# Last self-attention: V held still in the weighing, one group later, with one exponential per head

## The chip, the core and the metric

The kernel runs on one core of a Trainium2 chip. The metric is the device time of one execution in microseconds (us), the smaller the better. TensorE multiplies (PE in the rows, PEld its weight loads), VectorE is DVE, ScalarE is ACT, GpSimd is POOL and SyncE issues DMAs (SP).

## What is computed

A Perceiver block of two layers on x (128 batches of 32 tokens of 256 numbers): in each layer a cross-attention to a context of 257 tokens, a self-attention and a feed-forward part. The change touches only the second layer's self-attention (16 heads of 64, causal, rotary embedding), which the kernel runs in one stage with the quantised linear layer that ends the program:

```python
def _L1_attn_ref(x, W_qkv, W_out):          # x: (128, 32, 256), after a layer norm
    q, k, v = split(x @ W_qkv)              # 16 heads of 64
    q, k = rotary(q), rotary(k)
    scores = einsum('bqhd,bkhd->bhqk', q, k) / 8
    scores = where(tril, scores, -1e9)
    weights = softmax(scores)
    out = einsum('bhqk,bkhd->bqhd', weights, v)
    return out.reshape(b, s, 1024) @ W_out
x = x + _L1_attn_ref(_layernorm(x), ...)
x = x + _L1_ffn_ref(_layernorm(x), L1_ffn_weight)   # BitLinear: rounded rows times a ternary matrix
```

## The kernel before

The program is five stages, one after the other: cross-attention, self-attention with the router, experts, cross-attention, and the last stage (class `SelfAttention1`, from 1971 us of the profile to its end). Tokens lie on the 128 partitions, four batches of 32 in one group; there are G = 32 groups. The last stage walks over them in steps. Each engine has its own list of instructions, written out by hand in the methods `tensor`, `scalar`, `vector` and `gpsimd`, and meets the others only in semaphores, so an instruction that waits holds back all that stands behind it on its engine.

In the kernel before, step g holds: for group g, six projections to 512 columns (q in two halves, k in two, v in two; `project(g, i, c)`, each 6 products of 128 rows to 512 columns by way of `split_product`, L230), the rotary product (`rotate` on VectorE, three instructions at L2333 and L2336; the sum on GpSimd, L2407), the turning of the rotated q and k (`turn`, four transposes each, L2198) and copies of them by ScalarE (L2284); for group g-1 the scores (`scores`, L1131, 64 products in tiles of 64 rows by 32 columns of the array), the softmax and the weighing (`weigh`, L1180, in tiles of 32 by 32, the turned probabilities standing still and V streaming past in 64 columns); for group g-2 the turning of the result (`turn_out`, L2211), its split into a high and a low part (`attn_hi` on ScalarE, L2291, `attn_lo` on VectorE, L2345), and the output projection (`project_out`, 24 products of 256 columns, L230); and for older groups the BitLinear part: row statistics, rounding, two transposes (L2090) and two products (L2107), with `add` on VectorE (L2114). An f32 product appears in the trace as two matmuls, so 64 products are 128 records.

The softmax is all VectorE but for the exponential: two masked reads of the scores (L1151), the maximum (L1156), the subtraction (L1158), one exponential of 512 columns on ScalarE (L1137), the block transpose (L1164), the sums (L1165) and their reciprocal (L1171). After the weighing VectorE multiplies the 1024 columns of the result by the reciprocals (L2392, 1024 columns), and this is what `turn_out` waits for.

PSUM: two banks for the scores, two for the weighed result, and a ring of four banks for everything else. Whoever takes a bank of the ring waits until its last user but four takes ago has been read: `Ring.take` keeps that order, which is the order of the takes in `tensor`. Order of TensorE in a middle step before: q0, q1, turn_out 0, k0, k1, turn_out 1, turn q0, turn q1, scores(g-1), v0, turn k0, project_out(g-2), turn k1, v1, bit transposes, weigh(g-1), bit product. Layer norm of four groups is made ready in every fourth step (8 more transposes there).

## Time and profile before

| | us |
|---|---|
| median of three runs | 2590.14 |
| lowest, highest | 2585.91, 2591.77 |
| the profiled execution | 2589.96 |
| its span, first to last instruction | 2587.8 |
| mean granted TensorE clock of the span | 0.965 of full speed |
| scores of group 0 and of group 31 begin | 1996.7, 2549.3 |

The rows further down come from the profiled execution. A window row gives for a stretch its length, then the busy time and number of instructions of PE, PEld, DVE, ACT and POOL, the granted clock, the share of the DMA engines and GB/s. A group row gives the line, the engine, what is written from what, the shape, the count, the busy time and the mean length in ns, and behind the second bar the idle time of the engine before these instructions and what ended it. A timeline row gives start and length in us, and in brackets an idle time before it.

### The profile page before, as it was taken

The page shows a single profiled execution, that of the slowest core. Times are in us where ns is not written, and L with a number is a line of the kernel's source. Part 1 is how long each engine was busy: PE and PEld are TensorE (multiplying, and loading weights), DVE is VectorE, ACT ScalarE, POOL GpSimd, SP SyncE. Part 2 cuts the span into 40 slices and gives each one's busy share as a digit, 9 for nine tenths or more (in the row PEclk, how much of TensorE's full clock was granted, in tenths as well). Part 3 has the DMA queues.
Part 4 walks back from the last instruction along what each step waited for, and adds up shares of the span by engine and source line. Part 5 has one row for each costly group of instructions (what it writes and reads, how often), then busy time and mean ns, then how long its engine had stood idle before and what let it go on. Part 6 is the DMA issues. An engine that isn't in the chain of part 4 may idle for free. (4 is left out here: it accounts for less than half of the span.)

```text
span 2587.8 us, 103372 instructions
## 1 busy us (share of the span) xinstructions
PE 2402.1 (93%) x44640; PEld 1977.3 (76%) x44640; DVE 1813.0 (70%) x3820; ACT 1252.9 (48%) x2824; POOL 840.0 (32%) x740
## 2 busy tenths in 40 slices
PE   7999999999988857999995999999997999999997
PEld 6888888888855546888884777777776888888885
DVE  6778777777767663222225888888886788888886
ACT  5666666666544433333334777777763223232332
POOL 3333333332222112343435444444221323233231
PEclk9999999999998867999998999999998999999998
DMA  6545555554323253111115788888772000000000
GB/s 203 145 147 158 156 157 152 159 153 127 98 57 103 75 198 144 49 50 47 50 39 168 221 233 232 237 227 234 218 208 91 3 3 3 11 11 11 11 11 26
DMA packets 199554, 298.98 MB, mean 116 GB/s; under 512 B 29368, under 2 KB 107324, under 8 KB 197824
## 3 DMA queue, kind: packets, MB, share of 16 engines
q1 hardware_dynamic: 192288, 275.58, 36.0%
q0 software_dynamic: 6816, 16.79, 2.0%
q8 instruction: 356, 5.83, 1.0%
q14 instruction: 94, 0.77, 0.1%
HBM read 170.75 MB, written 78.77 MB: 96 GB/s over the span
## 5 line engine op out<-in xcount | busy, mean ns | idle before, releaser
L813 ACT ACTIVATE prob_x<-ps_score_x,neg_max_x 128x257 f32<-128x257 f32 x1024 | 402.6, 480 | 202.1 <-DVE neg_max_x L880 202.0
L880 DVE TENSOR_REDUCE neg_max_x<-ps_score_x 128x2 f32<-128x514 f32 x512 | 328.7, 683 | 109.8 <-PE ps_score_x L697 108.9
L708 PEld LDWEIGHTS ps_v_x<-v_wide_x,probT_x 128*32 128x32 f32 x18432 | 287.5, 108 | 129.3 <-issue 125.4
L708 PE MATMUL ps_v_x<-v_wide_x,probT_x 128*32 128x68 f32 x18432 | 335.0, 223 | 27.3 <-issue 23.1
L904 DVE STREAM_TRANSPOSE probT_x<-prob_x 128x1152 f32<-128x1152 f32 x256 | 343.8, 1343 | 0.0
L1049 POOL TENSOR_TENSOR ctxT_x_lo<-ready,ctxT_x_hi 128x514 fp32r<-128x514 f32 x128 | 152.9, 1195 | 387.0 <-ACT ctxT_x_hi L792 345.6
L2407 POOL TENSOR_TENSOR rot_s<-turned_s,swapped_s 128x512 f32<-128x512 f32 x128 | 164.5, 1297 | 328.0 <-DVE swapped_s L2336 288.2
L1049 POOL TENSOR_TENSOR split<-loaded,split 128x514 fp32r<-128x514 f32 x128 | 153.4, 1199 | 334.3 <-ACT split L792 319.9
L230 PE MATMUL ps_x<-split,w_q_x_hi 128*128 128x258 f32 x1024 | 208.5, 300 | 21.3 <-DVE w_q_x_lo L274 18.7
L230 PEld LDWEIGHTS ps_x<-split,w_q_x_hi 128*128 128x128 f32 x1024 | 160.0, 192 | 42.0 <-issue 25.9
L1947 DVE TENSOR_TENSOR hid_moe<-ps_up_moe,silu_moe 128x512 f32<-128x512 f32 x71 | 49.1, 691 | 203.5 <-PE ps_up_moe L230 203.5
L697 PE MATMUL ps_score_x<-kT_x,q_x 32*64 32x257 f32 x4096 | 178.2, 401 | 13.2 <-ACT prob_x L813 9.6
L804 ACT ACTIVATE kT_x<-ps_x,bias_k 128x257 f32<-128x257 f32 x256 | 122.1, 478 | 127.0 <-PE ps_x L230 126.5
L896 DVE STREAM_TRANSPOSE v_x<-ps_x 128x288 f32<-128x288 f32 x256 | 121.3, 479 | 74.6 <-PE ps_x L230 74.0
L230 PE MATMUL ps_x<-ctxT_x_hi,w_v_x_hi 128*128 128x258 f32 x512 | 159.0, 311 | 10.5 <-POOL ctxT_x_lo L1049 10.5
L230 PE MATMUL ps_x<-ctxT_x_hi,w_k_x_hi 128*128 128x258 f32 x512 | 146.4, 286 | 7.7 <-DVE v_x L896 7.7
L2291 ACT ACTIVATE attnT_s_hi<-ps_s 128x512 fp32r<-128x512 f32 x64 | 38.1, 599 | 231.4 <-PE ps_s L2211 231.4
L230 PE MATMUL ps_x<-split,w_q_x_lo 128*128 128x258 f32 x512 | 146.5, 286 | 0.0
L230 PE MATMUL ps_x<-ctxT_x_hi,w_v_x_lo 128*128 128x258 f32 x512 | 145.0, 283 | 0.0
L230 PE MATMUL ps_x<-ctxT_x_lo,w_v_x_hi 128*128 128x258 f32 x512 | 145.0, 283 | 0.0
L230 PE MATMUL ps_x<-ctxT_x_lo,w_k_x_hi 128*128 128x258 f32 x512 | 145.0, 283 | 0.0
L230 PE MATMUL ps_x<-ctxT_x_hi,w_k_x_lo 128*128 128x258 f32 x512 | 144.5, 282 | 0.0
(293 smaller groups left out, 6000.5 us busy)
## 6 DMA issues: line engine op xcount, KB each, us to landing
v_wide_x<-v_x SPq DMA_DIRECT2D x512, 76.5 KB, 2.1
v_out_x<-v_x SPq DMA_DIRECT2D x128, 306.0 KB, 4.2
v_wide_x<-v_out_x SPq DMA_DIRECT2D x512, 76.5 KB, 3.1
ready<-ctx SPq DMA_DIRECT2D x128, 257.0 KB, 3.6
loaded<-ctx SPq DMA_DIRECT2D x128, 257.0 KB, 4.2
gate_whole<-moe_experts SPq DMA_DIRECT2D x32, 256.0 KB, 3.8
lo_out<-gate_whole SPq DMA_DIRECT2D x32, 256.0 KB
w_moe<-lo_out SPq DMA_DIRECT2D x8, 1024.0 KB, 8.5
```

Source lines behind the costliest of these rows:

```text
L230: last = pe.do.matmul(out, a, b, start=n == 0, stop=n == len(steps) - 1)
L697: ins = pe.do.matmul(self.ps[m * 2 * T:(m + 1) * 2 * T, r, 0:S], q, self.kT[b % 3][rows, m, 0:S], start=True, stop=True)
L708: ins = pe.do.matmul(self.ps_v[r * T:(r + 1) * T, b % 2, :, :], self.probT[b % 3][:, r, n * T:(n + 1) * T], self.v_wide[b % 4][:, :, r, n, ...
L804: act.do.activation(out, src, ACT.Identity, bias=self.biases["k"][:, m:m + 1]).then_inc(*s.k.at(tag, b, m))
L813: act.do.activation(self.prob[b % 3][:, r, 0:S], self.ps[:, r, 0:S], ACT.Exp, bias=self.neg_max[b % 2][:, r:r + 1]).then_inc(*s.exp.at(tag ...
L880: dve.do.tensor_reduce(self.neg_max[b % 2][:, r], self.ps[:, r, 0:S], AX_X, ALU.max, negate=True).then_inc(*s.neg_max.at(tag, b, half))
L896: dve.do.transpose(out.rearrange("p x n d -> p n x d"), src.rearrange("p (n x d) -> p n x d", x=2, d=XD)).then_inc(*s.v.at(tag, b, m))
L904: dve.do.transpose(flat(self.probT[b % 3]), flat(self.prob[b % 3])).then_inc(*s.prob_T.at(tag, b))
L1049: pool.do.tensor_tensor(self.ctxT[b % 3].lo[:, :, 0:S], self.ctx_in[g % 2][:, j, :, :], self.ctxT[b % 3].hi[:, :, 0:S].bitcast(F32), ALU.s ...
L1947: dve.do.tensor_tensor(self.hid[t % 2][:, :], self.up_ps[t % 2][:, :], self.silu[t % 2][:, :], ALU.mult).then_inc(*s.hid.at(t))
L2291: act.do.activation(self.attnT.hi[:, c * 512:(c + 1) * 512], banks["attn", g, c][:, :], ACT.Copy).then_inc(*s.a_hi.at(g, c))
L2407: pool.do.tensor_tensor(self.rot[e][:, :, :], self.turned[e][:, :, :], self.swapped[e][:, :, :], ALU.add).then_inc(*s.r_rot.at(g, i, c))
```

## The change

- The softmax is cut in three. `mask` (VectorE) does the masked reads and the maximum. `exponent` (ScalarE) does one exponential per head, 16 of 32 columns, with the negative maximum as bias and with the sum of the head written out by the same call. `divide` (VectorE) takes the reciprocal of the sums, multiplies the 512 probabilities and does the block transpose. The subtraction (L1158), the sums (L1165) and the product over 1024 columns (L2392) are gone.
- `weigh` lets V stand still (32 rows by 64 columns) and streams the turned probabilities (32 columns): tiles of 32 by 64. Its result is already turned, so `turn_out` (eight transposes a step) is gone, and `attn_hi` and `attn_lo` read the weighed result itself.
- The weighed result of a group takes half of each of four banks; the other halves of two of these are the scores. So `mask` waits for the end of the weighing, and scores and reads of the result are kept apart by waits.
- Order: a step opens on TensorE with scores(g-1), then weigh(g-2), which was weigh(g-1) near the end of the step; then q0, q1, k0, k1, v0, turn q0, turn q1, project_out(g-2), turn k0, turn k1, bit transposes, v1, bit product. ScalarE and VectorE follow with their new lists. The ring of four banks is taken in the new order.
- The DMAs, the products of the projections and GpSimd's list are as before.

The diff, cut to its core:

```diff
@@ -1119,66 +1118,65 @@
         return a.rearrange("p (r n) -> p r n", r=self.order.R)
 
     def scores(self, pe, g, q_k):
-        s, tag, R = self.s, self.tag, self.order.R
+        s, R = self.s, self.order.R
         if g:
-            if self.bound is None:
-                pe.wait_ge(s.s_shift, tag, g - 1)
-            else:
-                pe.wait_ge(s.s_masked, g - 1)
+            pe.wait_ge(s.s_masked, g - 1)
         for heads, q, k in q_k(g):
             for b in range(BPG):
                 for r in range(R):
                     ins = pe.do.matmul(self.score[b * T:(b + 1) * T, r, heads, :], q(b, r), k(b, r), start=True, stop=True)
-        ins.then_inc(*s.s_score.at(tag, g))
+        ins.then_inc(*s.s_score.at("s1", g))
+
+    def mask(self, dve, g):
+        s, t, e = self.s, self.t, g % 2
+        dve.wait_ge(s.s_score, "s1", g)
+        if g >= 2:
+            dve.wait_ge(s.s_exp, "s1", g - 2)
+        for r in range(self.order.R):
+            ins = dve.do.scalar_tensor_tensor(out=self.cell(t["shifted"][e][:, :])[:, r], in0=self.score[:, r], scalar=self.scale,
+                                              in1=self.bound.unsqueeze(1).to_broadcast([P, self.order.NH, T]), op0=ALU.mult, op1=ALU.min)
+        ins.then_inc(*s.s_masked.at(g))
+        dve.wait_ge(s.s_masked, g)
+        dve.do.tensor_reduce(self.stat(t["neg_max"][e][:, :]), self.cell(t["shifted"][e][:, :]), AX_X, ALU.max, negate=True).then_inc(
+            *s.s_max.at("s1", g))
 
     def exponent(self, act, g):
-        s, tag, e = self.s, self.tag, g % 2
-        act.wait_ge(s.s_shift, tag, g)
-        act.do.activation(self.t["prob"][e][:, :], self.t["shifted"][e][:, :], ACT.Exp,
-                          scale=self.scale if self.bound is None else 1.0).then_inc(*s.s_exp.at(tag, g))
+        s, t, e = self.s, self.t, g % 2
+        act.wait_ge(s.s_max, "s1", g)
         if g >= 2:
+            act.wait_ge(s.s_probT, "s1", g - 2)
+            act.wait_ge(s.s_inv, "s1", g - 2)
+        for n in range(H):
+            own = slice(n * T, (n + 1) * T)
+            ins = act.do.activation(t["prob"][e][:, own], t["shifted"][e][:, own], ACT.Exp, bias=t["neg_max"][e][:, n:n + 1],
+                                    accum_out=t["sums"][e][:, n:n + 1])
+        ins.then_inc(*s.s_exp.at("s1", g))
+
+    def divide(self, dve, g):
+        s, t, e = self.s, self.t, g % 2
+        by_head = lambda a: a.rearrange("p (h q) -> p h q", q=T)
+        dve.wait_ge(s.s_exp, "s1", g)
+        dve.do.reciprocal(t["inv"][e][:, :], t["sums"][e][:, :]).then_inc(*s.s_inv.at("s1", g))
+        dve.wait_ge(s.s_inv, "s1", g)
+        dve.do.tensor_tensor(by_head(t["prob"][e][:, :]), by_head(t["prob"][e][:, :]),
+                             t["inv"][e][:, :].unsqueeze(2).to_broadcast([P, H, T]), ALU.mult).then_inc(*s.s_even.at(g))
+        dve.wait_ge(s.s_even, g)
         if g >= 2:
+            dve.wait_ge(s.s_pv, "s1", g - 2)
+        dve.do.transpose(t["probT"][e][:, :], t["prob"][e][:, :]).then_inc(*s.s_probT.at("s1", g))
 
     def weigh(self, pe, g, out, v, dv):
+        s, probT = self.s, self.t["probT"][g % 2]
+        pe.wait_ge(s.s_probT, "s1", g)
+        for n in range(H // 2):
+            for x in range(2):
+                h = 2 * n + x
+                c0 = self.order.column[h]
+                for b in range(BPG):
+                    rows = slice(b * T, (b + 1) * T)
+                    ins = pe.do.matmul(out[x * dv:(x + 1) * dv, b, n, :], v[rows, h * dv:(h + 1) * dv], probT[rows, c0:c0 + T],
+                                       start=True, stop=True)
+        ins.then_inc(*s.s_pv.at("s1", g))
 
...
         self.R = R = P // D1
-        order = HeadOrder(R, lambda r, n: n * R + r, lambda a: a.rearrange("p (n r) -> p r n", r=R))
-        ps_score = stack.enter_context(nc.psum_tensor(f"ps_score_{tag}", [P, R, 512], F32))
-        ps_out = stack.enter_context(nc.psum_tensor(f"ps_out_{tag}", [P, F1], F32))
+        order = HeadOrder(R, lambda r, n: n * R + r)
+        halves = stack.enter_context(nc.psum_tensor(f"ps_halves_{tag}", [P, BPG, 512], F32))
         self.banks = Ring([stack.enter_context(nc.psum_tensor(f"ps_{i}_{tag}", [P, 512], F32)) for i in range(4)])
-        self.out = ps_out[:, :].rearrange("p (h d) -> p h d", d=D1)
-        self.soft = SelfSoftmax(s, tag, order, self.t, ps_score[:, :, 0:order.NH * T].rearrange("p r (n q) -> p r n q", q=T),
+        self.out = halves[:, :, 256:512].rearrange("p b (n q) -> p b n q", q=T)
+        self.soft = SelfSoftmax(s, order, self.t, halves[:, 0:R, 0:order.NH * T].rearrange("p r (n q) -> p r n q", q=T),
...
+    def out_part(self, c):
+
+        return self.out[:, 2 * c:2 * c + 2, :, :]
+
+    def attn_part(self, t, c):
+
+        return t[:, :].rearrange("p (n b q) -> p b n q", n=H // 2, q=T)[:, 2 * c:2 * c + 2, :, :]
 
...
         def project_out(g):
             bank, emptied = banks.take(("o", g), s.s_x1, g)
-            pe.wait_ge(s.a_hi, g, self.NB - 1)
-            pe.wait_ge(s.a_lo, g, self.NB - 1)
+            pe.wait_ge(s.a_hi, g, 0)
+            pe.wait_ge(s.a_lo, g, 0)
             if emptied:
                 pe.wait_ge(*emptied)
             self.wout.await_split(pe)
...
             if g == 2:
                 self.bit.sum_weight(pe)
+            if before:
+                pe.wait_ge(s.r_qkT, g - 1, 1, self.NB - 1)
+                if g >= 3:
+                    pe.wait_ge(s.a_lo, g - 3, 0)
+                self.soft.scores(pe, g - 1, q_k)
+            if out:
+                pe.wait_ge(s.s_v, tag, g - 2, self.NB - 1)
+                self.soft.weigh(pe, g - 2, self.out, self.v[g % 2], D1)
             if now:
                 project(g, 0, 0)
                 project(g, 0, 1)
-            if out:
-                turn_out(g - 2, 0)
-            if now:
                 project(g, 1, 0)
                 project(g, 1, 1)
-            if out:
-                turn_out(g - 2, 1)
-            if now:
+                project(g, 2, 0)
                 turn(g, 0, 0)
                 turn(g, 0, 1)
-            if before:
-                pe.wait_ge(s.r_qkT, g - 1, 1, self.NB - 1)
-                self.soft.scores(pe, g - 1, q_k)
-            if now:
-                project(g, 2, 0)
-                turn(g, 1, 0)
             if out:
                 project_out(g - 2)
+            if now:
+                turn(g, 1, 0)
             if n < SG and j == 3:
                 for k in range(KD):
                     self.ln.turn(pe, n, k, banks)
             if now:
                 turn(g, 1, 1)
-                project(g, 2, 1)
             if 0 <= last < G:
                 self.bit.turn(pe, last)
-            if before:
-                pe.wait_ge(s.s_v, tag, g - 1, self.NB - 1)
-                if g >= 2:
-                    pe.wait_ge(s.s_out, tag, g - 2)
-                self.soft.weigh(pe, g - 1, self.out, self.v[(g - 1) % 2], D1)
+            if now:
+                project(g, 2, 1)
             if 0 <= last < G:
                 self.bit.product(pe, last)
 
...
         def attn_hi(g, c):
-            act.wait_ge(s.a_T, g, c)
+            act.wait_ge(s.s_pv, tag, g)
             if g:
                 act.wait_ge(s.a_o_ps, g - 1)
-            act.do.activation(self.attnT.hi[:, c * 512:(c + 1) * 512], banks["attn", g, c][:, :], ACT.Copy).then_inc(*s.a_hi.at(g, c))
+            act.do.activation(self.attn_part(self.attnT.hi, c), self.out_part(c), ACT.Copy).then_inc(*s.a_hi.at(g, c))
 
...
             if out:
+                attn_hi(g - 2, 1)
+                if before:
+                    act.wait_ge(s.s_masked, g - 1)
                 attn_hi(g - 2, 0)
-                attn_hi(g - 2, 1)
-            if now:
-                keep_turned(g, 0, 0)
-                keep_turned(g, 0, 1)
             if before:
                 self.soft.exponent(act, g - 1)
             if now:
                 keep_v(g, 0)
+                keep_turned(g, 0, 0)
+                keep_turned(g, 0, 1)
                 keep_turned(g, 1, 0)
             if n < SG and j == 3:
                 prepare(n)
             if now:
                 keep_turned(g, 1, 1)
-                keep_v(g, 1)
             if 0 <= last < G:
                 self.bit.keep_turned(act, last)
+            if now:
+                keep_v(g, 1)
...
         def attn_lo(g, c):
-            dve.wait_ge(s.a_T, g, c)
+            dve.wait_ge(s.s_pv, tag, g)
             if g:
                 dve.wait_ge(s.a_o_ps, g - 1)
             dve.wait_ge(s.a_hi, g, c)
-            at = slice(c * 512, (c + 1) * 512)
-            dve.do.tensor_tensor(self.attnT.lo[:, at], banks["attn", g, c][:, :], self.attnT.hi[:, at].bitcast(F32),
+            dve.do.tensor_tensor(self.attn_part(self.attnT.lo, c), self.out_part(c), self.attn_part(self.attnT.hi, c).bitcast(F32),
                                  ALU.subtract).then_inc(*s.a_lo.at(g, c))
 
...
+            if before:
+                if out:
+                    dve.wait_ge(s.s_pv, tag, g - 2)
+                self.soft.mask(dve, g - 1)
+            if out:
+                attn_lo(g - 2, 1)
             if now:
                 rotate(g, 0, 0)
+            if out:
+                attn_lo(g - 2, 0)
+            if now:
                 rotate(g, 0, 1)
             if g == 0:
                 self.wqkv[2].split_lo(dve)
-            if out:
-                attn_lo(g - 2, 0)
             if now:
                 rotate(g, 1, 0)
                 rotate(g, 1, 1)
-            if out:
-                attn_lo(g - 2, 1)
             if before:
-                self.soft.softmax(dve, g - 1)
+                self.soft.divide(dve, g - 1)
             if out:
                 dve.wait_ge(s.a_o_ps, g - 2)
                 dve.do.tensor_tensor(self.X[:, g - 2, :], self.X[:, g - 2, :], banks["o", g - 2][:, 0:D], ALU.add).then_inc(
...
                     self.bit.round_z(dve, done)
-            if before:
-                dve.wait_ge(s.s_pv, tag, g - 1)
-                dve.wait_ge(s.s_inv, tag, g - 1)
-                if g >= 2:
-                    dve.wait_ge(s.a_T, g - 2, self.NB - 1)
-                dve.do.tensor_tensor(self.attn[:, :].rearrange("p (h d) -> p h d", d=D1), self.out,
-                                     self.t["inv"][(g - 1) % 2][:, :].unsqueeze(2).to_broadcast([P, H, D1]), ALU.mult).then_inc(
-                    *s.s_out.at(tag, g - 1))
             if 0 <= last < G:
                 self.bit.add(dve, last)
 
```

## Rows read from the trace of the kernel before

**Rows 1.** the page: what each engine was busy of the whole span
```profile
PE 2402.1 (93%) x44640; PEld 1977.3 (76%) x44640; DVE 1813.0 (70%) x3820; ACT 1252.9 (48%) x2824; POOL 840.0 (32%) x740
```

**Rows 2.** a stretch of the last stage: us, busy per engine (count), clock, DMA
```profile
2300.00:2400.00 100.00, 99.91 (x1922) 87.50 (x1921) 82.87 (x182) 32.09 (x61) 31.44 (x26) 1.00 0.02 8
```

**Rows 3.** what TensorE waited for from 2000 to 2560 us: total, times, longest
```profile
PE ps_s L2211 <- DVE attn_s L2392: 4.0, 2, 3.0
```

**Rows 4.** one step of the last stage, cut where TensorE changes its work
```profile
2301.90:2303.12 1.22, 1.22 (x130) 1.18 (x129) 0.74 (x2) 0.81 (x2) 1.22 (x2) 1.00 0.02 7
2304.98:2307.90 2.92, 2.92 (x27) 2.92 (x26) 1.99 (x4) 1.60 (x3) 0.00 (x0) 1.00 0.00 0
2309.73:2310.04 0.31, 0.31 (x3) 0.14 (x1) 0.31 (x2) 0.11 (x1) 0.00 (x0) 1.00 0.00 0
2310.04:2311.96 1.92, 1.92 (x129) 1.83 (x128) 0.47 (x3) 0.76 (x2) 1.02 (x1) 1.00 0.03 9
2312.11:2314.98 2.87, 2.87 (x14) 2.29 (x13) 2.79 (x5) 0.00 (x0) 0.00 (x0) 1.00 0.00 0
2314.98:2315.34 0.36, 0.36 (x6) 0.36 (x4) 0.33 (x2) 0.00 (x0) 0.06 (x1) 1.00 0.00 0
2318.64:2319.61 0.97, 0.97 (x11) 0.80 (x9) 0.97 (x3) 0.77 (x2) 0.20 (x1) 1.00 0.00 0
2301.90:2319.61 17.71, 17.71 (x346) 15.43 (x345) 14.21 (x32) 5.25 (x11) 6.14 (x6) 1.00 0.01 2
```

**Rows 5.** groups of the last stage: line, shapes, count, busy, mean ns, idle
```profile
L2392 DVE TENSOR_TENSOR attn_s<-ps_out_s,inv_s 128x1024 f32<-128x1024 f32 x32 | 39.1, 1223 | 29.1 <-PE ps_out_s L1180 29.1
...
L1158 DVE TENSOR_TENSOR shifted_s<-shifted_s,neg_max_s 128x512 f32<-128x512 f32 x32 | 22.2, 693 | 1.1
...
L1137 ACT ACTIVATE prob_s<-shifted_s 128x512 f32<-128x512 f32 x32 | 20.3, 633 | 92.6 <-DVE shifted_s L1158 92.6
...
L1171 DVE RECIPROCAL inv_s<-sums_s 128x16 f32<-128x16 f32 x32 | 8.1, 253 | 1.1
```

**Rows 6.** timeline of the first self-attention: start, length, a 32*64 tiled group and the next
```profile
844.62 0.86 PE L1302 MATMUL ps_score_s<-kT_s,q_s 32*64 32x32 f32 x64
...
845.41 1.95 PE L1412 MATMUL ps_s<-router_moe,xT_moe 128*128 128x8 f32 x16
```

**Rows 7.** ScalarE groups of the whole program, by form
```profile
L804 ACT ACTIVATE kT_x<-ps_x,bias_k 128x257 f32<-128x257 f32 x256 | 122.1, 478 | 127.0 <-PE ps_x L230 126.5
...
L806 ACT ACTIVATE kT_x<-ps_x 128x257 f32<-128x257 f32 x256 | 95.0, 399 | 68.1 <-PE ps_x L230 64.2 <-issue 0.3
...
L1418 ACT ACTIVATE prob_moe<-logit_moe 128x32 f32<-128x32 f32 x8 | 1.8, 227 | 9.0 <-DVE logit_moe L1426 9.0
```

**Rows 8.** timeline of VectorE in the step of rows 4
```profile
2303.23 0.76 DVE L1151 SCALAR_TENSOR_TENSOR shifted_s<-ps_score_s,constants 128x256 f32<-128x256 f32 x2 [0.58 <-PE ps_score_s L1131]
...
2304.02 0.69 DVE L1156 TENSOR_REDUCE neg_max_s<-shifted_s 128x16 f32<-128x512 f32 x1
...
2308.11 0.42 DVE L2371 TENSOR_TENSOR X<-X,ps_s 128x256 f32<-128x256 f32 x1 [0.41 <-PE ps_s L230]
...
2312.10 1.22 DVE L2392 TENSOR_TENSOR attn_s<-ps_out_s,inv_s 128x1024 f32<-128x1024 f32 x1 [1.53 <-PE ps_out_s L1180]
...
2315.79 0.74 DVE L2336 TENSOR_TENSOR swapped_s<-ps_s,constants 128x256 f32<-128x256 f32 x2
...
2316.45 0.68 DVE L2345 TENSOR_TENSOR attnT_s_lo<-ps_s,attnT_s_hi 128x512 fp32r<-128x512 f32 x1
...
2317.05 0.68 DVE L2333 TENSOR_TENSOR turned_s<-ps_s,constants 128x512 f32<-128x512 f32 x1
...
2318.40 0.69 DVE L2333 TENSOR_TENSOR turned_s<-ps_s,constants 128x512 f32<-128x512 f32 x1
```

**Rows 9.** timeline of the end of the stage
```profile
2546.91 0.39 PE L2107 MATMUL ps_s<-wq_bit,zT_bit 128*128 128x256 bf16 x2
...
2562.69 0.55 PE L230 MATMUL ps_s<-w_out_s_hi,attnT_s_hi 128*128 128x256 f32 x1 [1.73 <-DVE attnT_s_lo L2345]
```

More of the change, by code:

```diff
@@ L166, in __init__ @@
             count("s_" + n, grid(SELF, g)) for n in ("score", "max", "shift", "exp", "probT", "inv", "pv", "out"))
-        self.s_sum = count("s_sum", grid(("s1",), g))
+        self.s_even = count("s_even", grid(g))
         self.m_xT, self.xn_left = count("m_xT", grid(s, k)), [
@@ L193, in __init__ @@
         self.s_masked = count("s_masked", grid(g))
-        self.a_T, self.a_hi, self.a_lo = (count("a_" + n, grid(g, half)) for n in ("T", "hi", "lo"))
+        self.a_hi, self.a_lo = (count("a_" + n, grid(g, (1, 0))) for n in ("hi", "lo"))
         self.a_o_ps, self.s_x1 = count("a_o_ps", grid(g)), count("s_x1", grid(g))
@@ L1100, with __init__ @@
 class HeadOrder:
-    def __init__(self, R, head, cells):
+    def __init__(self, R, head):
         self.R, self.NH = R, H // R
-        self.cells = cells
         self.column = {head(r, n): (r * self.NH + n) * T for r in range(R) for n in range(self.NH)}
 class SelfSoftmax:
-    def __init__(self, s, tag, order, tiles, score, scale, bound):
-        self.s, self.tag, self.order, self.t, self.score, self.scale, self.bound = s, tag, order, tiles, score, scale, bound
+    def __init__(self, s, order, tiles, score, scale, bound):
+        self.s, self.order, self.t, self.score, self.scale, self.bound = s, order, tiles, score, scale, bound
     def cell(self, a):
@@ L1173, in weigh @@
-    def weigh(self, pe, g, out, v, dv):
-        s, tag, probT = self.s, self.tag, self.t["probT"][g % 2]
-        pe.wait_ge(s.s_probT, tag, g)
-        for h in range(H):
-            c0 = self.order.column[h]
-            for b in range(BPG):
-                rows = slice(b * T, (b + 1) * T)
-                ins = pe.do.matmul(out[rows, h, :], probT[rows, c0:c0 + T], v[rows, h * dv:(h + 1) * dv], start=True, stop=True)
-        ins.then_inc(*s.s_pv.at(tag, g))
+        ins.then_inc(*s.s_score.at("s1", g))
@@ L2203, in q_k @@
             return [(n, at(self.qT, n), at(self.kT, n)) for n in range(self.soft.order.NH)]
-        def turn_out(g, c):
-            bank, emptied = banks.take(("attn", g, c), s.a_lo, g, c)
-            pe.wait_ge(s.s_out, tag, g)
-            if emptied:
-                pe.wait_ge(*emptied)
-            for n in range(4):
-                ins = pe.do.transpose(bank[:, n * P:(n + 1) * P], self.attn[:, c * 512 + n * P:c * 512 + (n + 1) * P], ident[:, :])
-            ins.then_inc(*s.a_T.at(g, c))
         def project_out(g):
             bank, emptied = banks.take(("o", g), s.s_x1, g)
-            pe.wait_ge(s.a_hi, g, self.NB - 1)
-            pe.wait_ge(s.a_lo, g, self.NB - 1)
+            pe.wait_ge(s.a_hi, g, 0)
+            pe.wait_ge(s.a_lo, g, 0)
             if emptied:
```

31 lines of the change are left out of this document (removed).

## Prediction

> **What bounds the kernel now.** I read the page first: TensorE is busy for 93% of the span and nothing else is near it [rows 1]. As a busy TensorE need not be a full one, I went to the stage that is changed: by stretches it is busy for 99.9 of 100 us, at the full clock, VectorE for 83 [rows 2], and in 560 us the longest wait behind one engine adds up to 4.0 us [rows 3]. The stage is thus a queue of TensorE work with no holes, and its length is the sum of what is in the queue. One step, cut where TensorE changes its work, gives that sum: 17.71 us, all of it busy [rows 4]. The steps on average are (2549.3 - 1996.7) / 31 = 17.83 us from scores to scores; every fourth holds eight more transposes, and the step cut here holds none, so my step is an ordinary one.
>
> So two questions decide: how much work leaves the queue, and whether the new order makes holes in it.
>
> **What leaves the queue.** The two `turn_out` groups go. One is four transposes between two projections, 0.36 us [rows 4]; two are 0.72 us.
>
> The weighing changes its shape. It takes 1.92 us for 128 matmuls now [rows 4], 15.0 ns each, in tiles of 32 by 32 with 64 streaming columns. The new shape (32 by 64 tiles, 64 columns standing, 32 streaming) is in the trace already: the scores of the first self-attention, 64 matmuls from 844.62 to the next group at 845.41, 0.79 us or 12.3 ns each [rows 6]. For 128 that is 1.58 us, 0.34 less. From both sides: the scores of the last stage, with 32 columns standing and 32 streaming, take 1.22 us for 128, 9.5 ns each [rows 4], which would be 0.70 less; at the other end nothing is gained, 1.92 us. I take 1.58, since the shape is the same.
>
> That stream of 32 columns costs less than one of 64 is what the rows say (9.5 and 12.3 ns against 15.0). A rule speaks against it: the Trainium skill, "TensorEngine Tiling (Array Packing)", section Performance Considerations, has it that each matmul bears about 60 cycles of overhead, so that a short stream is as long as one of 60 columns, and that one should not tile along a dimension that is already small. By that rule 32 columns cost what 64 cost and the weighing stays where it is; the trace doesn't agree for tiles that run side by side. What it would give is a rival below.
>
> Changes of tiling have a price too: before the scores, eight transposes take 0.97 us where eight by 0.36/4 would take 0.72, so about 0.25 for the way into tiles; before the weighing, two take 0.31 instead of 0.18, so 0.13 [rows 4]. There are two such entries now and two afterwards (into the scores, and from their tiles to those of the weighing), so I book no change; if the second cost nothing, 0.13 more would go, if twice, 0.13 less.
>
> Queue after: 17.71 - 0.72 - 0.34 = 16.65 us. With no holes, 1.06 us a step are gained.
>
> **What the new order may open.** I lay a step out from the start of the scores, t = 0. Scores until 1.22, entry 0.13, weighing 1.35 to 2.93. VectorE sees a weighing's end 0.14 us after its last matmul (it began at 2310.04, lasted 1.92, and L2392 began at 2312.10 [rows 4, 8]), so at 3.07 it may begin `mask`, which now waits for the weighing as well as for the scores. Behind `mask` on VectorE stand, in this order: `attn_lo`, `rotate`, `attn_lo`, three `rotate`, then `divide`. Their prices are starts to starts: the masked reads from 2303.23 to 2304.02, 0.79; the maximum 0.72 with the gap behind it; `attn_lo` 0.60; `rotate` (2317.05 to 2318.40) 1.35, or 1.26 where `attn_lo` follows, as it starts 0.66 after the swapped pair in place of 0.75 [rows 8]. Sum: 0.79 + 0.72 + 0.60 + 1.26 + 0.60 + 3 x 1.35 = 8.02, so the last rotation has been read at 11.1. ScalarE's `attn_hi` of 0.6 fit in between, as do GpSimd's sums.
>
> Who waits for that: `project_out`. The ring gives it the bank that k1 had four takes ago, which is free only when the last rotation has read it. TensorE gets there at 2.93 + 2.87 + 2.86 (k, taken as the q pair) + 1.44 (v0, half of 2.87) + 0.72 (two turns) = 10.82. A hole of 0.3 us opens in each step: the chain from the weighing through VectorE is longer by that than the five projections that cover it. It comes back each step, as both ends hang on the same weighing.
>
> After `project_out` (2.92, until 14.0) VectorE adds it to X (0.42, 0.2 after its end [rows 8]), and v1 waits for that, as its bank was `project_out`'s. The add ends at 14.7; v1 comes at 14.0 + 2 x 0.36 + 0.18 = 14.9. That holds by 0.2.
>
> The exponentials: one of 512 columns is 633 ns [rows 5], one of 32 is 227, and a bias from memory adds 478 - 399 = 79 ns [rows 7]. So 306 ns, without the sum that each must write out, which no row shows: between nothing and one more fixed part, 227 less 32 columns at (633 - 227)/480 ns, 200 ns. I take the middle, 0.41 us a head, 6.6 us for 16 (bounds 0.31 and 0.51: 5.0 and 8.1), against 0.63 before. `mask` ends at 4.6, so they end at 11.2 (12.7): VectorE comes to `divide` at 11.1. So they are hidden, by 1.5 us at the middle, for `divide` (0.25 + 0.69 + 0.71 and gaps, 1.75 us; L1171, the product as L1158 [rows 5]) must end before the add at 14.2. ScalarE's copies of v0 and of turned q, k stand behind them: 12.4 at the latest needed 14.0. If the cover is gone, each 0.1 us a head is 1.6 us a step.
> The Trainium skill, "ScalarE: Activation LUTs", section What ACT_TABLE_LOAD costs, gives 280 ns plus 0.833 per column with a pointer bias and an overlap of about 93 ns between neighbours: 214 ns a head, below my lower bound; no run here shows the sum written out.
>
> VectorE loses 693 (L1158), the sums, and 1223 ns (L2392), and gains a product like L1158 [rows 5]: its 14.21 busy us of the step [rows 4] become at most 13.0, so it isn't the bound on average. In every fourth step it also reads the two banks of the layer norm's transposes, and v1's bank is then the first of these: turned at 15.1, copied by ScalarE behind the turned k (as L2345's source is now, 0.6), read by VectorE like `attn_lo` (0.7), 16.5 at the latest, where v1 would come at 14.9 + 8 x 0.09 = 15.6. I estimate 0.8 us there, 0.2 a step.
>
> Period: 16.65 + 0.3 + 0.2 = 17.15 where the same mean reads 17.71 before: 0.56 a step.
>
> **The ends.** Steps 1 to 31: 31 x 0.56 = 17.4; one weighing leaves them for the end, 1.9. Start: v0 now stands ahead of the turns and waits for its weight's low part; -1. End: from the last middle product to the last `project_out` passed 2562.69 - 2546.91 = 15.8 us [rows 9]. After: entry and scores 1.5, entry and weighing 1.7, seen 0.14, `mask` 1.5, exponentials 6.6, now bare, `divide` 1.75, then the add, statistics and rounding of VectorE's list, which outlast the last weighing (an estimate without rows: 3.9 in all), two `attn_lo` 1.3: 18.4, so -2.6. Sum: 17.4 + 1.9 - 1 - 2.6 = 15.7, about 16 us. Against the profiled execution, 2589.96 (span 2587.8, 2.2 around it), that is 2574; the median of the runs is 2590.14, the same.
>
> **Rivals.**
> A, no hole: VectorE keeps up, or the weighing is nearer to 9.5 ns. 31 x (1.06 to 1.42) = 33 to 44, less 2: 2548 to 2559. For it: the hole is 0.3 of 8 us, within what the gaps may vary. Against: the rotation rows are very regular.
> B, the weighing stays at 1.92 (the rule on short streams): 31 x 0.34 = 10.5 less gain, 2584.5. Against it, rows 6.
> C, slower: the exponentials become the bound. VectorE's `divide` waits for them, the add waits behind it, and v1 for the add. v1 begins at 4.6 + 16e + 1.75 + 0.5. At e = 0.51 us this is 15.0, just hidden; with e = 0.59 it is 16.3, which uses up the gain; so 0.59 us a head is the point from which it decides. At 0.65: 17.25, 2.3 later than 14.9, so 31 x (2.3 - 0.56) = 54 slower at most, plus 4 at the end: 2648; at 0.60, about 2595. For it: the output of the sum has no row. Against it: it would have to cost over 280 ns, more than a whole exponential of 32 columns.
> D, the hole is larger, about 0.9 us (mask or reads across banks slower, or VectorE's long fourth steps push the next `mask`): 31 x 0.5 = 16 lost, 2590, no change.
>
> **Numbers.** Forecast 0.42 (2564 to 2584), A 0.18, B 0.12, C 0.14, D 0.14. A measurement of this kernel tells 0.2%, 5 us, from no change. Faster: forecast, A, half of B and a little of D, 0.70; same: the rest of B and most of D, 0.15; slower: C and a bit of D, 0.15. The range of 8 in 10 takes the upper part of A, all of B and D and the start of C: 2555 to 2594.
>
> **What would show it.** Right: `turn_out`'s rows gone; scores to scores about 17.3 on average; the weighing near 12.3 ns a record; `project_out` (L230) waiting for VectorE's swapped product about 0.3 us a step; exponentials near 0.4 us a head and no wait of `divide` for them. Wrong: `divide` waiting for ScalarE for over 1.5 us a step, a weighing at 15 ns, or TensorE waiting at v1 for X in every step. A granted clock under 1.00 in the stage would say that the holes cost more than their length.

## The result, and the profile after

The changed kernel takes 2642.83 us (median of four runs, 2633.37 to 2655.28) against 2590.95 us for the kernel before (2585.91 to 2600.04, four runs): 1.0209 times as long, 95% interval 1.0184 to 1.0234. It is slower, by about 52 us, where 2574 was forecast; whether by more than 2% the interval leaves open. The profiled execution took 2642.49 us, with a span of 2640.7.

The page of the changed kernel, engines busy of the span and the queues that bring instructions (packets, MB, share of the DMA engines); it answers to [rows 1]:

```profile
PE 2394.9 (91%) x44384; PEld 1963.5 (74%) x44384; DVE 1768.3 (67%) x3756; ACT 1395.4 (53%) x3816; POOL 852.2 (32%) x740
...
q8 instruction: 354, 5.80, 1.0%
```

Work did leave TensorE: 256 records fewer and 7 busy us less. It is in the idle time that the 52 us lie. The last stage by stretches, columns as in [rows 2]:

```profile
2000.00:2100.00 100.00, 88.67 (x1682) 75.78 (x1682) 68.04 (x151) 53.09 (x229) 34.42 (x26) 0.95 0.01 3
2100.00:2200.00 100.00, 89.77 (x1684) 76.69 (x1682) 66.01 (x153) 48.77 (x204) 30.76 (x24) 0.91 0.01 2
2200.00:2300.00 100.00, 88.10 (x1702) 74.99 (x1701) 70.99 (x162) 50.64 (x210) 29.68 (x22) 0.97 0.02 8
2300.00:2400.00 100.00, 90.72 (x1733) 77.14 (x1732) 72.08 (x166) 51.18 (x211) 29.72 (x22) 0.95 0.04 13
```

Three columns matter against [rows 2]. TensorE was busy 99.91 of 100 us and is now busy 88 to 91; the granted clock was 1.00 (2.4 GHz throughout) and is now 0.91 to 0.97, so part of each stretch ran at 1.2 GHz. VectorE fell from 83 to about 70, so it isn't the new bound.

What TensorE waited for in the last stage, from 2000 to 2700 us (in total, times, longest); it answers to [rows 3], where the largest entry was 4.0 us:

```profile
PE ps_halves_s L1177 <- issue: 53.8, 30, 2.3
PE ps_s L2088 <- DVE xn_bit L2080: 5.3, 1, 5.3
PE ps_s L2105 <- ACT zT_bit L2096: 4.3, 9, 0.5
PE ps_s L230 <- issue: 4.1, 3, 2.9
PE ps_s L230 <- DVE swapped_s L2328: 3.3, 13, 0.3
```

L1177 is the weighing's product. In 30 steps TensorE stands still inside it, 1.8 us on average, and not for another engine: "issue" means that nothing in the profile held it back. The wait that I had forecast is the last row, and small; the second and third are the end of the stage.

One such place in the timeline of TensorE (start, length, idle time in brackets; the rows between are projections):

```profile
2322.08 1.29 PE L1127 MATMUL ps_halves_s<-loaded 64*32 64x32 f32 x128
2323.30 0.33 PE L1177 MATMUL ps_halves_s<-probT_s,loaded 32*64 32x32 f32 x13
2324.89 1.37 PE L1177 MATMUL ps_halves_s<-probT_s,loaded 32*64 32x32 f32 x115 [1.26 <-issue]
...
2334.53 0.36 PE L230 MATMUL ps_s<-w_out_s_hi,attnT_s_hi 128*128 128x256 f32 x1 [0.25 <-DVE swapped_s L2328]
```

The scores run through; behind them the weighing does 13 records, stands still, and does the other 115. Since `mask` now waits for the weighing, VectorE waits with it (timeline of VectorE, the same step):

```profile
2326.30 0.76 DVE L1136 SCALAR_TENSOR_TENSOR shifted_s<-ps_halves_s,constants 128x256 f32<-128x256 f32 x2 [3.15 <-PE ps_halves_s L1177]
```

Where the 52.9 us of span went, by the starts of the scores of group 0 and 31 (1996.70 and 2549.35 before; 1992.35 and 2598.34 after): the 31 steps took 606.0 us in place of 552.65, 53.3 more; what follows took 42.4 in place of 38.4, 3.9 more; what precedes took 4.3 less. The start of group 0's scores lies between 1988.5 and 1999.5 in the six kernels that are alike up to there (the changed one, e1, e2, e3, e7 and e8 below), so of the start I read nothing. A step is 19.55 us on average; 17.83 before, 17.27 by the forecast (which set 17.15 against a step of 17.71, 0.56 less).

### The profile page after: what moved, and what is told of

The parts are those of the page before. It is cut to its first block and busy times, and to the rows that moved or that the text cites. A ratio compares the mean times of both kernels' runs of the same rounds, so it can differ in the third digit from the quotient of the medians.

```text
span 2640.7 us, 103712 instructions
## 1 busy us (share of the span) xinstructions
PE 2394.9 (91%) x44384; PEld 1963.5 (74%) x44384; DVE 1768.3 (67%) x3756; ACT 1395.4 (53%) x3816; POOL 852.2 (32%) x740
## 5 line engine op out<-in xcount | busy, mean ns | idle before, releaser
L2395 POOL TENSOR_TENSOR rot_s<-turned_s,swapped_s 128x512 f32<-128x512 f32 x128 | 176.3, 1387 | 417.7 <-DVE swapped_s L2328 354.8
L697 PE MATMUL ps_score_x<-kT_x,q_x 32*64 32x257 f32 x4096 | 178.0, 402 | 14.2 <-ACT prob_x L813 10.6
L1151 ACT ACTIVATE prob_s<-shifted_s,neg_max_s 128x32 f32<-128x32 f32 x512 | 156.7, 307 | 7.4 <-DVE neg_max_s L1140 3.5
```

Source lines behind the costliest of these rows:

```text
L697: ins = pe.do.matmul(self.ps[m * 2 * T:(m + 1) * 2 * T, r, 0:S], q, self.kT[b % 3][rows, m, 0:S], start=True, stop=True)
L1151: ins = act.do.activation(t["prob"][e][:, own], t["shifted"][e][:, own], ACT.Exp, bias=t["neg_max"][e][:, n:n + 1], accum_out=t["sums"][e] ...
L2395: pool.do.tensor_tensor(self.rot[e][:, :, :], self.turned[e][:, :, :], self.swapped[e][:, :, :], ALU.add).then_inc(*s.r_rot.at(g, i, c))
```

## A first reading: where the stops stand

Two theories were open.

F: TensorE runs out of fetched instructions. Each small product is two instructions of TensorE's list, a weight load and a matmul, and an f32 product is two records of each kind, so scores and weighing are 128 + 128 records each, 512 instructions in a row. In the old order long projections stood between the two.

G: it is the change of tile form (64 by 32 for the scores, 32 by 64 for the weighing, in the same PSUM banks) that stops the array where the two touch.

For F two counts speak. From 2000 to 2620 us, 36 gaps of over 0.8 us lie between the starts of two neighbouring TensorE instructions of one line. Three are among the turns at the stage's start. The other 33 all lie at the same place, if TensorE's instructions are numbered through the whole trace in order of time: at number 193 of a block of 256, and 256, 512 or 768 instructions apart. The block and the step have no common length, which is why the stop comes after 13 records in one step and elsewhere in another. And the instruction queue moves blocks of that size. The pages of the kernel before and of e4 below, whose TensorE list is 8192 instructions longer:

```profile
q8 instruction: 356, 5.83, 1.0%
```

```profile
q8 instruction: 388, 6.36, 1.0%
```

The traces hold 91297 TensorE instructions before, 90803 after, 86835 in e3 and 99489 in e4. Divided by 256 that is 356.6, 354.7, 339.2 and 388.6; the pages show 356, 354, 339 and 388 packets of 16.4 KB. So one packet is 256 TensorE instructions. The packets' own records around the step above (start in us, length in ns, bytes):

```
2307.71  1198  16384
2322.59   945  16384
2326.39   876  16384
```

The stop ended at 2324.89, 2.3 us after its packet had begun. The same holds for all 33: from the start of the last packet to the end of the stop passed 2.16 to 2.86 us, median 2.59; in e4, for the 32 up to the same time, 2.32 to 2.93, median 2.44. The bound is sharp and holds without a stop too. With blocks and packets both numbered from the start of the trace, the instruction behind number 193 of block n never begins sooner than 2.16 us after the start of packet n - 1, in any of the 867 blocks of the last stage in the ten traces on record; in the changed kernel number 193 itself began as early as 0.2 us before that packet. So what stands behind number 193 comes with that packet, and TensorE stops where the packet comes too late. Undisturbed, the weighing works off 256 instructions in 1.27 us. G has no reason for any of these numbers. The kernel before shows the same thing in the small: four gaps of over 0.8 us between 2000 and 2620 us, all four at instruction 193 of a block, two of them in the scores. Its waits of TensorE had, one line under the one in rows 3, from 2000 to 2560 us:

```profile
PE ps_score_s L1131 <- issue: 2.6, 2, 1.4
```

## The experiments

**e1: two projections between scores and weighing.** The changed kernel, with q0 and q1 moved:

```diff
                 self.soft.scores(pe, g - 1, q_k)
+            if now:
+                project(g, 0, 0)
+                project(g, 0, 1)
             if out:
                 pe.wait_ge(s.s_v, tag, g - 2, self.NB - 1)
                 self.soft.weigh(pe, g - 2, self.out, self.v[g % 2], D1)
             if now:
-                project(g, 0, 0)
-                project(g, 0, 1)
```

> The changed kernel with one move: the two q projections (12 products, 2.87 us) stand between the scores and the weighing on TensorE. Theory F (TensorE runs out of fetched instructions: scores and weighing are 512 of them in 2.7 us): the stop inside the weighing goes, the wait called issue before it falls from 51.8 us to under 10, the weighing lasts about 1.45 us in every step. VectorE's mask still waits for the weighing and so begins 2.9 us later, which opens a hole of about 3.1 us before project_out: steps of about 19.7 us, total near 2650. Theory G (the stop comes from changing tiles, or from scores and results sharing banks): the stop stays at 1.8 us a step beside the hole, steps of about 21.3 us, total near 2700.

Measured, in one run as for e2 to e4, e7 and e8: 2680.08 us (the kernel before beside it 2592.61). TensorE's waits from 2000 to 2700 us:

```profile
PE ps_s L230 <- DVE swapped_s L2329: 36.6, 55, 1.2
PE ps_s L2202 <- POOL rot_s L2396: 21.2, 31, 0.8
PE ps_s L2202 <- DVE swapped_s L2329: 8.4, 28, 0.9
PE ps_halves_s L1127 <- issue: 6.2, 4, 2.1
...
PE ps_halves_s L1177 <- issue: 4.8, 4, 1.9
```

The stop in the weighing is all but gone (53.8 to 4.8 us; the 51.8 of the expectations is the same wait up to 2600 us), and 28 of 32 weighings take 1.27 us from first to last matmul start. So it was not in the weighing's form or banks by themselves but in what stood directly ahead of it; that two forms touch there is ruled out only by e4. The total lies between what the theories said, 2650 and 2700, and settles nothing, since `mask` still waits for the weighing, which now comes 3 us later: the rotations behind it on VectorE release banks and GpSimd's sums late, and 66 us of holes open there; the step is 20.71 us, not 19.7. That I had under-priced.

**e2: the old form of the weighing, in the new place.**

```diff
...
-                    ins = pe.do.matmul(out[x * dv:(x + 1) * dv, b, n, :], v[rows, h * dv:(h + 1) * dv], probT[rows, c0:c0 + T],
...
+                ins = pe.do.matmul(to, probT[rows, c0:c0 + T], v[rows, h * dv:(h + 1) * dv], start=True, stop=True)
```

> The changed kernel, but the weighing in its old form (tiles of 32 by 32, probabilities standing, 64 columns of V streaming), still right behind the scores; its result is laid out wrongly, so the output is not the reference's. 256 instructions as before. F: the stop stays in most steps, shorter by the 0.3 us that the slower weighing gives the fetch, 1.2 to 1.6 us a step on average. G (the 32 by 64 form or the shared banks by row tile): the stop is gone and the weighing lasts 1.78 us in each step; total near 2600.

Measured: 2641.98 us, the time of the changed kernel. TensorE's first wait from 2000 to 2700 us:

```profile
PE ps_halves_s L1176 <- issue: 45.5, 30, 1.9
```

30 stops again, with other tiles, 1.5 us each in place of 1.8, as F had said. The weighing's own work takes 0.5 us more here (at the least 1.77 us where it is 1.27 in the new form), but with the stop it takes 3.46 us on average against 3.22: about half of what the new form gains goes into a longer stop. The step, 19.31 us, is none the longer, and here the granted clock has a part. With as many stops it was 0.98 to 1.00 from 2100 to 2500 us, where the changed kernel had 0.91 to 0.97; why is open. Two of its stretches:

```profile
2100.00:2200.00 100.00, 90.36 (x1707) 77.22 (x1707) 71.61 (x161) 51.53 (x215) 34.39 (x26) 1.00 0.01 3
2200.00:2300.00 100.00, 91.39 (x1722) 78.15 (x1721) 72.68 (x167) 51.58 (x212) 30.78 (x23) 1.00 0.02 8
```

**e3: half of the heads weighed.**

```diff
-        for n in range(H // 2):
+        for n in range(H // 4 if g else H // 2):
```

> The changed kernel with the weighing of half the heads left out from group 1 on (the output is not the reference's): scores and weighing are 384 instructions in a row instead of 512. F: the stops get rarer and shorter, under half of 51.8 us of issue wait in all. G: each change of tiles still costs its 1.8 us, the issue wait stays near 50 us. The work left out is 0.7 us a step: total near 2575 by F, 2615 by G.

Measured: 2588.25 us, a step of 17.83. TensorE's waits:

```profile
PE ps_halves_s L1177 <- issue: 27.2, 15, 2.4
PE ps_halves_s L1127 <- issue: 6.6, 5, 1.8
```

384 instructions in a row still stop, 15 times in the weighing and 5 times in the scores, and as long as before in the weighing (1.8 us). F had said rarer, shorter and under half of 51.8 us: rarer they are, shorter they aren't, and 33.8 us in all is over half. The total lies between 2575 (F) and 2615 (G), nearer to F. G, with 1.8 us at every change of form, has no room for the 17 weighings without a stop. A shortage in blocks has: it matters whether the dense stretch holds the place behind number 193 of a block, and the stop there is as long as the packet is late.

**e4: the kernel before, each product of the last scores issued twice.** Here no tile form changes inside the group, and the weighing is where it was.

```diff
-        for heads, q, k in q_k(g):
+        for heads, q, k in [x for x in q_k(g) for _ in range(2)]:
```

> The kernel before, with each product of the last stage's scores issued twice in a row (same result): 512 instructions in 2.4 us, all of one tile form, no shared banks, nothing else of the change. F: a stop of 1.5 to 2.3 us appears inside the scores in most steps: 32 x (1.2 + 1.9) = 99, total near 2690. G: no stop, 32 x 1.2 = 38 for the work, total near 2628.

Measured: 2727.3 us. Waits of TensorE, and one group of scores in the timeline:

```profile
PE ps_score_s L1131 <- issue: 69.2, 34, 2.7
PE ps_s L2211 <- DVE attn_s L2392: 4.0, 2, 3.0
```

```profile
2333.93 1.54 PE L1131 MATMUL ps_score_s<-loaded 64*32 64x32 f32 x158
2337.71 1.03 PE L1131 MATMUL ps_score_s<-loaded 64*32 64x32 f32 x98 [2.24 <-issue]
```

The old kernel stops the same way as soon as it has 512 small instructions in a row, by 2.0 us a time. G expected no stop and 2628 us; F 2690. A step became 21.98 us for 1.22 us of added work (17.83 + 1.22 = 19.05). F stands, and its size was too small: of the 2.9 us beyond the work, 69.2 us over 32 steps, or 2.2, are the stops, where F had 1.9; F had no term for the clock either, which fell to 0.95 to 0.98 here.

**e5: the changed kernel in another order.** Scores, v0, q0, weighing, q1, k0, k1. `mask` reads the scores while v0 and q0 run, and the weighing waits for the mask's reads instead of the reverse, so the wait is turned round and the two dense groups are apart. ScalarE does half of the exponentials ahead of `attn_hi` and half behind.

```diff
+            if now:
+                if g:
+                    project(g, 2, 0)
+                project(g, 0, 0)
             if out:
                 pe.wait_ge(s.s_v, tag, g - 2, self.NB - 1)
+                if before:
+                    pe.wait_ge(s.s_masked, g - 1)
                 self.soft.weigh(pe, g - 2, self.out, self.v[g % 2], D1)
...
             if before:
-                if out:
-                    dve.wait_ge(s.s_pv, tag, g - 2)
                 self.soft.mask(dve, g - 1)
```

> The changed kernel re-ordered: a step opens with the scores, then the first v projection and the first q projection (2.9 us), then the weighing, then the other three projections. The mask reads the scores while these two projections run, and the weighing waits for it in place of the other way round; ScalarE does 8 exponentials before the weighing's end and 8 after. By the hand layout project_out then comes at 11.0 us of a step with its bank free at 10.4, no hole. F: no stop, steps of 16.4 to 16.9 us against 19.5 of the changed kernel and 17.8 of the kernel before, granted clock back to 1.00 in the stage: total 2545 to 2565, faster than both. G: the stop of 1.8 us a step stays: 2600 to 2615.

Measured: 2574.4 us (2568.05 to 2578.03, four runs) against 2590.24: 0.9927 times, interval 0.9904 to 0.9949: 0.7% faster. F had said no stop, steps of 16.4 to 16.9 and 2545 to 2565 us; five stops remained in the weighing, 4.5 us, three in the scores, 2.5 us, and the step came to 17.46.

**e6: the same with three projections between.** v0, q0 and q1, and the lists of ScalarE and VectorE moved to suit.

```diff
                 project(g, 0, 0)
+                project(g, 0, 1)
             if out:
...
             if now:
-                project(g, 0, 1)
                 project(g, 1, 0)
```

> e5_woven with three projections instead of two between scores and weighing (v, q, q; 4.3 us), ScalarE doing 12 exponentials before the weighing's end, and VectorE rotating both q halves before it reads the weighed result. F: 512 instructions in a row now take at least 6.7 us wherever a piece of 256 begins, against 5.3 in e5_woven; the few stops left there (8.7 us inside scores and weighings) go, total 2560 to 2570 if no new hole opens; VectorE's last reads before project_out are 0.0 to 0.3 us late by the layout, 2570 to 2575 if they bind. G: no change from e5_woven.

Measured: 2566.79 us (2564.98 to 2567.2, four runs) against 2589.17 (2582.74 to 2597.11, seven): 0.9906 times, interval 0.9877 to 0.9935. This is within what F said, 2560 to 2570, and it beats both kernels, the one before by 0.9%. Two stretches of the stage, one weighing, and TensorE's waits:

```profile
2200.00:2300.00 100.00, 98.56 (x1912) 82.68 (x1899) 82.66 (x183) 55.45 (x229) 34.00 (x28) 1.00 0.02 8
2300.00:2400.00 100.00, 97.46 (x1888) 81.98 (x1887) 83.70 (x179) 57.40 (x244) 32.95 (x26) 1.00 0.02 8
```

```profile
2301.91 1.49 PE L1179 MATMUL ps_halves_s<-probT_s,loaded 32*64 32x32 f32 x128
```

```profile
PE ps_s L2090 <- DVE xn_bit L2082: 5.3, 1, 5.3
PE ps_s L231 <- DVE attnT_s_lo L2346: 4.9, 1, 4.9
PE ps_s L2107 <- ACT zT_bit L2098: 4.3, 9, 0.5
PE ps_halves_s L1128 <- issue: 3.2, 4, 1.4
```

All 32 weighings run through in 1.27 us (one in 1.32), TensorE is busy again for 98 of 100 us, and the clock is back at 1.00. The step is 17.20 on average, an ordinary one 16.8. The same 44384 records as in the changed kernel, in another order, are thus worth 76 us. That is the worth of two things together, the distance between the dense groups and the turned wait of `mask`; e1 has the first alone and is slower, and the second alone was not run. What is left stands at the end (the first three rows) and in the first step, 20.5 us.

**e7: no sums beside the exponentials.** This and e8 are about the other engines.

```diff
-            ins = act.do.activation(t["prob"][e][:, own], t["shifted"][e][:, own], ACT.Exp, bias=t["neg_max"][e][:, n:n + 1],
-                                    accum_out=t["sums"][e][:, n:n + 1])
+            ins = act.do.activation(t["prob"][e][:, own], t["shifted"][e][:, own], ACT.Exp, bias=t["neg_max"][e][:, n:n + 1])
...
```

`divide` takes the reciprocal of the maxima in place of the missing sums.

> The changed kernel without the sums written out by ScalarE's exponentials (the division takes another number, so the output is not the reference's). The rival that ScalarE became the bound (16 exponentials with 16 accumulator reads, 4.9 us a group): each group gets 1.4 us or more shorter on ScalarE, and the total falls by up to 45 us. F: ScalarE is hidden in all steps, only the end of the stage gets 1 to 2 us shorter: total 2632 to 2645, stops as before.

Measured: 2638.12 us, inside the changed kernel's own four runs (2633.37 to 2655.28), and 52.9 us of stops as before. The exponentials of one group in ScalarE's timeline here, and then, in the changed kernel's, one head's exponential, the read of its sum, and the next head's exponential:

```profile
2324.29 3.50 ACT L1151 ACTIVATE prob_s<-shifted_s,neg_max_s 128x32 f32<-128x32 f32 x16
```

```profile
2328.13 0.30 ACT L1151 ACTIVATE prob_s<-shifted_s,neg_max_s 128x32 f32<-128x32 f32 x1
2328.34 0.19 ACT L1151 ACTIVATION_READ_ACCUMULATOR prob_s<-shifted_s,neg_max_s 128x1 f32 x1
2328.43 0.31 ACT L1151 ACTIVATE prob_s<-shifted_s,neg_max_s 128x32 f32<-128x32 f32 x1
```

From start to start a head takes 0.213 us without the sum and 0.306 with it, in all 32 groups; 16 heads take 3.5 and 4.9 us. 1.4 us less a group on ScalarE bought nothing on TensorE, where 45 us of total were possible had it been the bound: the exponentials are not.

**e8: the divide's product kept away from GpSimd's sum.** In the changed kernel that product (L1161) took 691 to 1822 ns, mean 1117, where L1158 of the same size took 693 [rows 5]. A wait for GpSimd's last rotary sum was put ahead of it:

```diff
         dve.wait_ge(s.s_inv, "s1", g)
+        if g + 1 < G:
+            dve.wait_ge(s.r_rot, g + 1, 1, 1)
         dve.do.tensor_tensor(by_head(t["prob"][e][:, :]), by_head(t["prob"][e][:, :]),
```

> The changed kernel with one wait more: VectorE's product of the probabilities begins only when GpSimd has done the last rotary sum of the step. If the product's 1117 ns mean (691 at least) comes from running beside GpSimd's sum, which also reads two SBUF tensors, it now takes about 0.69 us in every step and GpSimd's sum 1.30. F: this isn't what costs the time; the total stays within 10 us of 2642, as the product is behind project_out's last operand.

Measured: 2655.81 us. The product's group here, and the same group in the changed kernel:

```profile
L1163 DVE TENSOR_TENSOR prob_s<-prob_s,inv_s 128x512 f32<-128x512 f32 x32 | 22.2, 693 | 87.3 <-POOL rot_s L2397 87.3
```

```profile
L1161 DVE TENSOR_TENSOR prob_s<-prob_s,inv_s 128x512 f32<-128x512 f32 x32 | 35.7, 1117 | 1.1
```

Alone it takes 693 ns every time. So the length was contention between VectorE and GpSimd. Keeping them apart saves 13.5 us of VectorE and costs it 87.3 us of waiting, so the overlap is the better bargain for VectorE. For the total nothing is shown: 2655.81, beyond the 10 us that F allowed, is one run, and the changed kernel's four reach 2655.28.

## Why the prediction was wrong

The sign was wrong, and the step that failed is the one with which the sum begins and ends: that the stage's length is "the sum of what is in the queue", and with it the price of putting scores and weighing side by side. I booked two entries into tiles as before and counted the new neighbourhood at nothing. From first to last matmul start the weighing takes 3.22 us on average where it takes 1.27 undisturbed, so the neighbourhood costs 1.95 us a step. I read the queue as work, and never as a list that has to be brought in.

The bookkeeping of a step: forecast 17.27 on average; the weighing up to the next group's start 3.37 (3.22 and 0.15) where 1.58 stood, +1.79; the sum is 19.06; measured 19.55. The 0.49 left has one visible candidate, the granted clock: about 0.94 over the stage and 1.00 in the forecast. In 16.9 us of work about 1 us would be lost if all of it went by the clock, an estimate from the stretches above; and e6, with the stops gone, has its clock at 1.00 and a step of 17.20. How the 0.49 is made up is not shown. Nor is it the number of stops alone that sets the clock: over the steps of the stage it was 0.96 in e4 and 0.97 in e3, which have stops, 0.96 in e1, whose holes are mostly waits for VectorE and GpSimd, but 0.99 in e2 with its 30 stops. The prediction did say that a granted clock under 1.00 would mean that holes cost more than their length.

The other steps, in its order:

- Two `turn_out` groups gone, 0.72 us: right. TensorE has 256 records fewer.
- The weighing at 12.3 ns a record, 0.34 us gained, with 0.70 as the outer bound: the direction was right, the size short. Undisturbed it takes 1.27 us from first to last matmul start where the old form takes 1.78, in every one of 32: 0.51 gained, 10.0 ns a record. The slip was in the reading of rows 6: of their 0.79 us, 0.64 lie between the first and the last start (10.2 ns a record) and 0.15 behind the last, once for a group; doubling the whole counted that end twice. Rival B, in which the weighing stays at its old length by the rule of the Trainium skill on short streams ("TensorEngine Tiling (Array Packing)", section Performance Considerations), is out: 32 columns in tiles of 32 by 64 cost 10.0 ns a record where 64 in tiles of 32 by 32 cost 14.0. The tile form differs too, so columns alone were not tested.
- The hole at `project_out`, 0.3 us, for VectorE's swapped product: right in place and size, 0.25 us in the timeline above, as the layout from the weighing's end says, but not in number. It appears in 13 steps, 3.3 us in all, where every step was booked. Rival D, a larger one, is not there.
- v1 waiting for X "holds by 0.2": it holds. No such wait is among the listed ones; in e8, which delays VectorE, it appears (4.0 us, 16 times).
- The exponentials at 0.41 us a head between 0.31 and 0.51, hidden: they are hidden, and 0.306, the lower bound, so the 0.10 added for the sum was too much. The sum's price, which no row had shown, is 0.306 - 0.213 = 0.093 us a head, though its own instruction has 187 ns in the trace: in part it overlaps with its neighbours. What the lower bound had left out is that two exponentials without a sum overlap, by as much. VectorE waited for them once, 3.9 us, at the end. Rival C is out. Its threshold was wrong by its own formula: v1 would be later than 14.9 by the gain of 0.56 at 0.54 us a head already, not 0.59, and 0.60 would give about 2620 us, not 2595. The slack of the exponentials was also 1.25 us (14.2 - 1.75 - 11.2) and not 1.5. Neither mattered at 0.306. The figure from the Trainium skill ("ScalarE: Activation LUTs", section What ACT_TABLE_LOAD costs), 214 ns a head, is met by e7 (213) and not by the kernel with its sums.
- "A product like L1158": 1117 ns in place of 693. I took the price from a place where GpSimd was idle. No harm from it is seen: VectorE was busy for 70 of 100 us.
- The end: forecast 2.6 us more, measured 3.9 more, though cut otherwise (from the last scores on). TensorE's waits there for VectorE's `xn_bit`, 5.3 us, and ScalarE's `zT_bit`, 4.3 us, are not the difference, as the kernel before has them too, 5.3 and 3.8. New are one more stop of the weighing, 2.0 us, and two holes ahead of `project_out` of 2.9 us each, where the kernel before had waits of 0.5, 3.0 and 1.7.

With the stops gone the layout was a good one. The changed kernel has one step whose weighing had no long stop, from 2085.73 to 2102.64, 16.91 us; it holds no BitLinear part yet and a stop of 0.7 us among its projections (at 2090.65), so 16.2 of work. In e6 such early steps take 16.04, ordinary ones 16.8; the forecast had 16.95 for an ordinary one, 0.17 of it the weighing that came out shorter. And e6's total, 2566.79, lies 7 us under what the prediction gave for this change: the gain was there, behind an order that the list's supply allows. That order is another one than was predicted, so e6 doesn't make the forecast right.

The range of 2555 to 2594 and the 0.15 for slower were built from rivals which all were waits between engines or prices of work. None was a limit of TensorE itself, though the waits of before had two stops of the scores by "issue", rows 4 had the counts (129 weight loads and 130 matmuls in 1.22 us) and the page of before the 356 packets.

What stays open: how many blocks TensorE holds ahead and what makes it ask for the next. Two projections between the dense groups left five stops of the weighing in e5, three left none in the weighing and four in the scores; one alone was not tried. So no distance is claimed beyond these.

## What to carry to other kernels

Before moving small tiled products next to each other, count instructions as well as time: 256 in a row went through at full speed in most steps here (the scores of the kernel before stopped in 2 of 32), 512 stopped for about 2 us in nearly every step, in two kernels and with three tile forms. Put long products between such groups, and turn a wait round, if need be, so that the reader works while these run. When the profile shows "issue" as the releaser inside a group of one line, look whether the stops are whole blocks of instructions apart before looking for a semaphore.

## What the hardware showed that I had not expected

- TensorE's instructions come in packets of 16.4 KB, 256 each; a stop for want of them ended 2.16 to 2.95 us after the start of its packet, in all ten traces, and stood behind instruction 193 of a block in the count of the trace.
- Stops of 1.8 us in steps of 19.5 went with a granted clock of 0.91 to 0.97 in the stretches of the stage; without them it was 1.00. Stops of 1.5 us in steps of 19.3 (e2) left it at 0.98 to 1.00 from 2100 to 2500 us.
- VectorE's product of two operands slows down where GpSimd's sum of two may run beside it: 693 ns kept apart (e8), 1117 in the mean and up to 1822 otherwise. The sum lengthens too, 1384 ns in the mean against 1293 in e8.
- A sum written out by ScalarE shows 187 ns as an instruction and adds 93 ns to the pace of 213.
